# Graph network on one core: a pair's last sums turned after two chunks of the next pair, and the edge counts of layer 1 made after the next reading of sums

## What is computed

```
# layer 0
agg = segment_sum(x[src], dst, 6250)
h = (1.0 + eps) * x + agg
h = relu(batch_norm(h @ W1 + b1, g1, be1))      # 512 -> 1024
h = relu(batch_norm(h @ W2 + b2, g2, be2))      # 1024 -> 512
x = layernorm(x + (x + h))
# layer 1
agg = segment_sum(x[src], dst, 6250)
indeg = segment_sum(ones, dst, 6250)
h = where(indeg > 0, agg, x)
h = batch_norm(relu(h @ W.T + b), gamma, beta)
x = layernorm(x + h)
```

## Time and profile before

| what | value |
|---|---|
| median of 3 runs | 2598.41 us (2590.33 to 2599.28) |
| profiled execution, its time | 2596.4 us |
| profiled execution, its span | 2594.7 us |
| PE busy | 2309.4 us, 89% |
| POOL busy | 1604.1 us, 62% |
| DVE busy | 1361.8 us, 52% |
| ACT busy | 796.0 us, 31% |
| mean granted clock of PE | 0.942 |

### The profile page before, as it was taken

One profiled execution on the slowest core, in us unless ns is written; L12 is line 12 of the kernel. 1 busy time (PEld: TensorE's weight loads), 2 busy tenths in 40 slices (PEclk: granted clock), 3 DMA queues, 4 the chain that ended last, 5 costly groups with the idle time before them and its releaser, 6 DMA issues. The chain is left out here.

```text
span 2594.7 us, 41691 instructions
## 1 busy us (share of the span) xinstructions
PE 2309.4 (89%) x9657; PEld 1514.8 (58%) x9658; DVE 1361.8 (52%) x2155; ACT 796.0 (31%) x1272; POOL 1604.1 (62%) x1729
## 2 busy tenths in 40 slices
PE   3999999999999999799995299999999999999964
PEld 2666666666666666688884255555555555555544
DVE  5555555555555455433336655545545555554557
ACT  1233333333333333455548411111111111111147
POOL 6777777777777777100002467777777777777712
PEclk9999999999999999899996699999999999999976
DMA  7777777777777777332217767777777777777748
GB/s 254 221 237 241 224 246 237 231 242 218 242 240 231 247 223 248 101 111 93 89 55 228 254 190 219 212 226 217 224 222 213 222 222 215 225 224 215 224 136 286
DMA packets 180571, 545.11 MB, mean 210 GB/s; under 512 B 48787, under 2 KB 51178, under 8 KB 175794
## 3 DMA queue, kind: packets, MB, share of 16 engines
q0 software_dynamic: 125120, 410.09, 53.3%
q1 hardware_dynamic: 33880, 78.23, 10.0%
q10 hardware_dynamic: 21544, 56.48, 6.5%
HBM read 493.06 MB, written 51.62 MB: 210 GB/s over the span
## 5 line engine op out<-in xcount | busy, mean ns | idle before, releaser
L767 PE MATMUL psum<-ring,select 128*125 x2600 | 1272.5, 613 | 12.3 <-issue 8.6
L542 POOL DMA_INDIRECT ring<-x_in,staged x782 | 799.2, 1022 | 249.7 <-issue 223.7
L542 POOL DMA_INDIRECT ring<-x_d,staged x782 | 750.2, 959 | 261.7 <-issue 223.0
L767 PEld LDWEIGHTS psum<-ring,select 128*125 128x125 f32 x2600 | 483.5, 192 | 383.6 <-issue 338.2
L638 DVE TENSOR_TENSOR rows_lo<-ring,rows_hi 128x512 fp32r<-128x512 f32 x500 | 327.5, 688 | 281.2 <-ACT rows_hi L854 279.3
L854 ACT ACTIVATE rows_hi<-ring 128x512 fp32r x500 | 289.4, 623 | 418.2 <-SPq L518 282.1
L795 PE MATMUL psum<-sumsT_hi,w_hi 128*128 128x250 f32 x1248 | 401.1, 321 | 4.3 <-DVE sumsT_lo L661 4.3
L752 PE MATMUL psum<-rows_hi,select_r 128*125 128x512 f32 x500 | 380.9, 762 | 7.1 <-DVE rows_lo L638 3.6
L795 PE MATMUL psum<-sumsT_lo,w_hi 128*128 128x250 f32 x1248 | 350.5, 281 | 0.0
L795 PE MATMUL psum<-sumsT_hi,w_lo 128*128 128x250 f32 x1248 | 348.9, 280 | 0.0
L795 PEld LDWEIGHTS psum<-sumsT_hi,w_hi 128*128 128x128 f32 x1248 | 237.9, 191 | 36.0 <-issue 32.6
(11 more groups left out here) (161 smaller groups left out, 2257.0 us busy)
## 6 DMA issues: line engine op xcount, KB each, us to landing
hidden_d<-hidden ACTq DMA_DIRECT2D x25, 1000.0 KB
act_f<-hidden_d SPq DMA_DIRECT2D x24, 1000.0 KB
ring<-x_in,staged POOLq DMA_INDIRECT x782, 3.8
ring<-x_d,staged POOLq DMA_INDIRECT x782, 3.7
own<-x_in ACTq DMA_DIRECT2D x50, 224.0 KB
own_r<-x_in SPq DMA_DIRECT2D x10, 1120.0 KB
own<-x_d ACTq DMA_DIRECT2D x50, 224.0 KB
own_r<-x_d SPq DMA_DIRECT2D x10, 1120.0 KB
```

Of the source, the lines that this page charges most:

```text
L542: nc.gpsimd.indirect_dma_start(slot(s), None, table, bass.IndirectOffsetOnAxis(ap=staged[:, s:s + 1], axis=0)).then_inc(gathered[s], 16)
L767: whole = nc.tensor.matmul(agg(h), select[h][:, WHOLE_AT.index(p), :], of_chunk(pe, first, place), start=False, stop=n + 1 == WINDOW, skip ...
```

## The change

On PE, the pair no longer starts with both clears and the turn. Only bank 0 is cleared at first. Then the first two chunks of the new pair's first tile are added into bank 0, and behind them come the clear of bank 1 and the turn of the last pair's sums (`between`). The register `cleared` chooses which bank column is cleared there.

On DVE, the counts of edges leave `selection` and become a function `counts`. In layer 1 the counts of tile 0 are made after `low_part`, and those of tile 1 after `read_sums` of tile 0, ahead of the remainders of tile 1's split chunks.

```
-                    if layer == 1:
-                        dve.wait_ge(select_done[h], 2 * v + 2)
-                        with nc.allow_low_precision(reason="counts up to WINDOW are exact in bfloat16"):
-                            nc.vector.tensor_reduce(edge_count[h][:, 0, :], ...
-                            nc.vector.tensor_reduce(edge_count[h][:, 1, :], ...
+
+                def counts(v, h):
+                    dve.wait_ge(select_done[h], 2 * v + 2)
+                    with nc.allow_low_precision(reason="counts up to WINDOW are exact in bfloat16"):
+                        nc.vector.tensor_reduce(edge_count[h][:, 0, :],
+                                                select_r[h][:].bitcast(F32).rearrange("p k n -> p n k"), AX.X, ALU.add)
+                        nc.vector.tensor_reduce(edge_count[h][:, 1, :], select[h][:].rearrange("p k n -> p n k"),
+                                                AX.X, ALU.add).then_inc(counted[h], 1)
...
                         read_sums(v, tiles(pair, 1), 1)
                         low_rows(v, 0, first[0], 0, 2)
                         low_part(v)
+                        if layer == 1:
+                            counts(v, 0)
                         low_rows(v, 0, first[0], 2, 5)
                         selection(v, 1, tiles(i, 1), first[1])
                         low_rows(v, 0, first[0], 5, SPLIT)
 
                         read_sums(v, tiles(i, 0), 0)
+                        if layer == 1:
+                            counts(v, 1)
                         low_rows(v, 1, first[1], 0, 4)
...
-                def clear(i, h):
-                    pe.wait_ge(sums_done[h], i * groups + 1)
-                    nc.tensor.matmul(agg(h)[:, 0:1], m.zeros[:, 0:z.NT], m.ones[:, 0:1],
-                                     start=True, stop=False, skip_group_check=True)
+                def clear(out):
+                    nc.tensor.matmul(out, m.zeros[:, 0:z.NT], m.ones[:, 0:1], start=True, stop=False,
+                                     skip_group_check=True)
...
                     for n, p in enumerate(ORDER):
+                        if n == 2:
+                            between()
...
-                def turn(job):
+                def turn(job, bank=None):
+
                     pe.wait_ge(lo_done, 2 * job + 1)
                     for h in range(2):
                         pe.wait_ge(sums_done[h], job + 1)
+                    if bank is not None:
+                        at = within(pe, bank * m.BANK, 2 * m.BANK, "bank 1 or 2")
+                        clear(m.psum[0:z.NT, bass.ds(at, 1)])
...
                 with pe.Fori(0, z.PAIRS) as i:
-                    clear(i, 0)
-                    clear(i, 1)
+                    pe.wait_ge(sums_done[0], i * groups + 1)
+                    clear(agg(0)[:, 0:1])
+                    pe.reg_mov(cleared, 1)
                     with pe.Fori(0, groups) as g:
                         v = of_use(pe, i, groups, g)
-                        turn(v)
-                        scatter(i, v, g, tiles(i, 0), 0)
-                        scatter(i, v, g, tiles(i, 1), 1)
+
+                        scatter(i, v, g, tiles(i, 0), 0, lambda: turn(v, pe.snap(cleared, min_val=1, max_val=2)))
+                        scatter(i, v, g, tiles(i, 1), 1, lambda: None)
+                        pe.reg_mov(cleared, 2)
```

More of the change, by code:

```diff
@@ L734, in agg, with scatter @@
                     return m.bank(h)[0:z.NT, :]
-                def clear(i, h):
-                    pe.wait_ge(sums_done[h], i * groups + 1)
-                    nc.tensor.matmul(agg(h)[:, 0:1], m.zeros[:, 0:z.NT], m.ones[:, 0:1],
-                                     start=True, stop=False, skip_group_check=True)
-                def scatter(i, v, g, tile, h):
+                def clear(out):
+                    nc.tensor.matmul(out, m.zeros[:, 0:z.NT], m.ones[:, 0:1], start=True, stop=False,
+                                     skip_group_check=True)
+                def scatter(i, v, g, tile, h, between):
                     tile_use = pe.snap(2 * v + h)
@@ L808, in _ @@
                                      start=True, stop=False, skip_group_check=True).then_inc(counts_zeroed, 1)
+                cleared = pe.alloc_register(f"pe_cleared{layer}")
                 with pe.Fori(0, z.PAIRS) as i:
-                    clear(i, 0)
-                    clear(i, 1)
+                    pe.wait_ge(sums_done[0], i * groups + 1)
+                    clear(agg(0)[:, 0:1])
+                    pe.reg_mov(cleared, 1)
                     with pe.Fori(0, groups) as g:
                         v = of_use(pe, i, groups, g)
-                        turn(v)
-                        scatter(i, v, g, tiles(i, 0), 0)
-                        scatter(i, v, g, tiles(i, 1), 1)
+                        scatter(i, v, g, tiles(i, 0), 0, lambda: turn(v, pe.snap(cleared, min_val=1, max_val=2)))
+                        scatter(i, v, g, tiles(i, 1), 1, lambda: None)
+                        pe.reg_mov(cleared, 2)
                 uses = pe.snap(groups * z.PAIRS)
@@ L1387, in gnn_kernel @@
         m.bank = lambda b: psum[:, b, :]
+        m.psum, m.BANK = psum[:].rearrange("p b c -> p (b c)"), 512
         m.banks = lambda a, b: psum[:, a:b, :]
```

## The result

The changed kernel takes 2674.44 us (median of 4 runs, 2673.45 to 2675.61) against 2595.23 us before (4 runs). The ratio is 1.0298, with a 95% interval of 1.0281 to 1.0315: slower by about 79 us. The forecast was 2681.

What follows compares the result with a forecast made beforehand. Gathers bound layer 0 and the PE program layer 1. From 2596.4 us, less 2, 5, 43.2 and 14.4, plus 105.5 for counts and 42.5 for clock, gave 2679.8, stated as 2681; range 2648 to 2708.

Steps and rivals of the forecast that it cites:

- What bounds the kernel: Layer 0 bound by gathers, about 41.4 us a pair at least; layer 1 by the PE program, 39.51 us a pair.
- Part 1, the borders: Between pairs, two whole chunks cover PE's bank 1 wait: 1.8 us per border plus 0.6 clock; layer 0 gains 2 us.
- Part 2, the start of layer 1: Tile 0's counts moved after `low_part`: free inside the loop, first split chunk of layer 1 5 us earlier (bounds 3 and 7).
- Part 3, the counts of tile 1: Layer 1, ahead of tile 1's remainders: DVE's 4.22 us of counts land wholly on PE, 25 times, 105.5 us.
- The clock: Half clock on PE behind nearly every layer 1 stop: 1.7 us each (bounds 0 and 3.4), 42.5 us in all.
- The rival with the loss held to 1 us: Layer 1 stops: low spell lies half in the stop, costing about 1 us each; 2664 us (2655 to 2668), chance 0.12.
- the case of no loss: Layer 1: clock stays up after stops, or falls for less; 2638 us with no loss, 2638 to 2655, chance 0.08.
- The sum: Whole kernel: 2596.4 - 2 - 5 - 43.2 - 14.4 + 105.5 + 42.5 = 2679.8 us, 2681 as a median.
- Counts hidden behind PE: Layer 1: PE reaches the split chunk late enough that counts do not hold it; 2575 to 2590 us, chance 0.02.
- No change: Whole kernel: gain and loss cancel if a stop costs 2.6 us a pair in place of 5.9; 2596 us, chance 0.03.

Runs made afterwards that it cites:

- the filled stop: Changed kernel plus 18 needless 500-column matmuls on PE in tile 1 of each layer 1 pair, ahead of its wait for the first remainder: 2623.11 us.

## Why the prediction was right

- *What bounds the kernel.* It held. Layer 0 did not follow PE's gain (688 gathers in 910 us), and the experiment with the old turn in layer 0 bears this out. Layer 1 follows PE as long as PE needs more than 39.2 us a pair. With 39.51 us it stood just above that, which is why taking work off PE's border alone brought 11 us and not 58.
- *Part 1, the borders.* The mechanism was right; the term was too small. 1.8 us of gain per border measured 3.15 - 0.86 = 2.3 us, since the transposes start with no switch time ahead of them and the first split chunk overlaps their end. 24 x 0.5 = 12 us more were gained. The low clock behind the borders went as well: with the turn and without the stops, PE's own work is 36.7 us a pair, which is 39.5 less 2.3 and 0.6, to 0.1 us. In layer 0, 2 us were forecast and layer 0 ended 3.9 us sooner; its turn measured 5 to 6 us in all. What I had not foreseen there is a new wait of PE for remainders of its split chunks (38.4 us in 130:1040 of the changed kernel, 35 times). It is a wait for gathers at one remove. ACT must have the rows before it rounds them for DVE, and ACT's wait for landings in that stretch rose like this, before and after:

```profile
ACT rows_hi L854 <- SPq L518: 144.8, 89, 4.9
...
ACT rows_hi L866 <- SPq L518: 265.8, 178, 4.9
```

POOL waits for PE there never longer than the 0.3 us that it idles ahead of each gather anyway, so the new wait delays no gather.

- *Part 2, the start of layer 1.* 5 us were forecast for the first split chunk. Counted from layer 1's first gather, that chunk came 3.8 us sooner and the first whole chunk 6.4.
- *Part 3, the counts of tile 1.* 4.22 us per stop were forecast; PE's weight load shows 4.14 more than before and PE itself stands 4.28, and one more of the larger sum made the stop 3.8 us longer. The chain had no slack, as the 0.97 us had said.
- *The clock.* Taken at 1.7 us per stop, it is 2.05 by the filled stop; 51 us in place of 42.5. The layer's granted clock fell further than forecast too, to 0.94 and not 0.96: the low spell is about 6.8 us behind some stops and 3.4 behind others, as the three pairs above show. Part of it lies in the stop itself and costs nothing, 1.7 us in the one shown. The rival with the loss held to 1 us had named this, but priced the loss too low, and it fell with the case of no loss. The Trainium skill, "TensorE: Matmul & The Clock Gate", section "What's actually happening", puts the penalty for warming up under 1% of a typical kernel's span. Applied to all the stops of this kernel, as the prediction did beside its sum, that is too low: 51 us are 1.9% of 2674.
- *The sum.* A pair was forecast to grow by 4.22 + 1.7 - 1.8 - 0.6 = 3.52 us, and it grew by 3.52. That this agrees to the last digit is luck: two terms were too small in opposite directions, 12 us at the borders and about 9 in the clock, and nearly cancelled. Between the profiled executions the forecast was 83.4 us and 78.9 were measured. Up to the first split chunk of layer 1, 8.6 us were gained (1496.65 - 1488.05) where 7 were forecast: 3.9 in layer 0, 0.9 from its end to layer 1's first gather, 3.8 behind that. From there to the same chunk of the last pair, 84.6 us were lost, and 84.5 were forecast. What follows took 2.8 us more where 5.9 were forecast for the last stop. It took 5.0 more up to the last chunk, and 2.1 less in the last stage, which the change does not touch. The other 2 of the 6.6 us between 2681 and 2674.4 come from the step from the profiled execution to the median.
- *The rivals.* Counts hidden behind PE would have needed 4.2 us of slack; they had none. No change would have needed a stop that costs 2.6 us a pair; it cost 4.28 and 2.05. POOL's waits rose by 82 us in 20 pairs, 4 us a pair where 3 were forecast.

## What to carry to other kernels

A piece of work on an engine that is half idle is free only at some places of its program. Look at what stands next in that engine's queue, and whether the bounding engine already waits for it: a wait of 0.97 us there said that each further microsecond would be paid in full. The same two instructions one step later cost nothing.

Price a stop of PE by its length and by the clock behind it: here a stop of 4.3 us brought 2.05 us more. And before work is taken off an engine, look at how far the next bound is. PE stood at 39.5 us a pair, the gathers at 39.2. For the same reason the effects of two halves of a change need not add up: the turn was worth 11 us alone and some 80 beside the misplaced counts.

## What the runs showed of the hardware

Needless matmuls in a stop made the kernel 51 us faster, as the granted clock of layer 1 stayed at 1.00 in place of 0.94. With the counts alone, stops and old borders together, layer 1 ran at 0.93, and its pair took 46 us where the stop and the old border explain 43.1: there the clock cost nearly 3 us a pair.

In one batch the same program took 3119 us where it takes 2592 to 2596 elsewhere, while each gather was issued in the usual 0.95 us and its packets took nearly the usual time. The ratios of the four kernels in it lay between 0.989 and 1.005, where they are 0.995 to 1.063 otherwise. A comparison in such a stretch says little; its cause stays open.
